# A selective scan on one core: order of the last-column copies, and a re-ordered opening of the stage

## The chip, the cores and the metric

The kernel runs on one core of a Trainium2 chip. The metric is the device time of one execution in microseconds (us). It was run three times: median 2136.71 us, from 2136.35 to 2136.91.

## The reference

A block of four layers over an input `x` of 4 × 1024 tokens of 128 features in float32; each adds its result to `x` and begins with a layer norm: windowed attention, a mixture of experts, a two-layer selective state-space model ("mamba"), and the mixture of experts once more. The change is in the third:

```python
def _mamba_layer(x, W_in, conv_w, conv_b, W_x, W_dt, b_dt, A_log, Dvec, W_out):
    xz = jnp.einsum('bld,ed->ble', x, W_in)
    u, z = jnp.split(xz, 2, axis=-1)                 # 256 channels each
    u = _silu(_causal_conv1d(u, conv_w, conv_b))     # 4 taps
    x_dbl = jnp.einsum('bld,rd->blr', u, W_x)
    dt, Bm, Cm = jnp.split(x_dbl, [DT_RANK, DT_RANK + D_STATE], axis=-1)
    dt = jax.nn.softplus(jnp.einsum('blr,dr->bld', dt, W_dt) + b_dt)
    A = -jnp.exp(A_log)                              # 16 states a channel
    # h_t = exp(dt A) h_(t-1) + dt B_t u_t ;  y_t = C_t h_t + D u_t
    y = _selective_scan(u, dt, A, Bm, Cm, Dvec)
    y = y * _silu(z)
    return jnp.einsum('bld,od->blo', y, W_out)
```

## The kernel before

**Units and steps.** `mamba()` cuts the work into 16 units: layer (2) × 512 tokens (`SEG`) × batch row (4), two units to a batch row, in the order of `UNITS`. The first three units are of the lower layer, then upper and lower alternate, and the last three are of the upper one. A unit holds its 256 channels as two halves `h` of 128 partitions. It has 16 steps, one for each state `n`; step `G` = 16 U + n. The second unit of a batch row starts from the last column that the first left for each state: `keep(U, n)` on ScalarE (L2174) copies the last columns of states n and n+1 out of the ring of 4 state buffers. So 8 of the 16 units (0, 1, 3, 5, 6, 8, 11, 13) keep columns, eight copies each.

**One step, by engine.** Each engine has its own hand-written order and waits for counting semaphores.
- VectorE: for each half a scan (`tensor_tensor_scan`, L2367) from a decay and a drive term, and for the driven states a product (L2347) for the next state's drive, in PSUM. Before the scans of step G it waits until state G−4 has been read by GpSimd and, in a unit that keeps columns, until the `keep` of state G−4 has been done. At step 4 (`BACK`) it makes the gating product of the unit before (L2372).
- ScalarE: exponentials `decays` (L2123), the copies out of PSUM, the softplus, the SiLU with a load of its table before and behind, and `scale` (L2146). In each step its order is: decays, copy of Y (step 3, L2153), convolution copies (steps 2 and 4, L2053), SiLU (step 4), the rows' copies (step 6), `soft` (step 9), gate copies (`gated`, L2110), `scale`, columns, and `keep` last.
- TensorE: the rows of B spread over the partitions (`rows_b`, L1865), or for 5 of the states the transposes of what ScalarE scaled (`upright`, L1890), or the diagonal form (state 11); the sum over states as transposes into Y (`accumulate`, L1919), which waits for GpSimd's product; for the next unit the convolution (L1823), gates (L1855), steps and transposes. The drive terms have two PSUM buffers (`PB`).
- GpSimd: the product of each state with C (L2313), two drives a unit for the states 4 and 12 (L2300), two products for the next unit's steps (L2321, L2324), and in units 0 to 5 the addition of the input.
- SyncE issues the transfers of B and C rows through DRAM.

**States by kind.** `AWAY` (4, 12): drive from GpSimd, decay in PSUM. `ACROSS` (2, 5, 8, 10, 14): scaled by ScalarE in the transposed layout and turned upright by TensorE. `DIAGONAL` 11. The eight others are driven: rows by TensorE, product by VectorE. `nth_drive`, `nth_upright`, `nth_across` and the lists `uses0` and `uses1` (who uses the two side banks, in order) count semaphores.

**The opening.** Before the loop, ScalarE takes the square root for the layer norm (`deviations`), the exponential of `decay`, the copies of unit 0's rows (`round_high(0)`), the softplus, and the first decays; TensorE the first rows, both gates, turns of B and delta_u, and half a convolution of unit 1.

## Time and profile before

| | us | share of the span |
|---|---|---|
| median of three runs | 2136.71 | |
| profiled execution | 2136.81 | |
| its span, first to last instruction | 2134.9 | |
| TensorE busy | 2000.8 | 94% |
| VectorE busy | 1473.7 | 69% |
| GpSimd busy | 1440.3 | 67% |
| ScalarE busy | 1205.7 | 56% |
| scan stage (first to last scan) | about 777 to 1575 | 37% |

The shares are means over stages with different limits; the stage in question has to be looked at by itself. Profile lines name the engine (PE TensorE, PEld its weight loads, DVE VectorE, ACT ScalarE, POOL GpSimd, SP SyncE), the line of the kernel (L2367), the operation, and what it writes and reads; many small buffers live in one tile called `experts`. In square brackets stands the idle time of the engine ahead of the group and what the profile takes for its releaser. Starts are counted from the span's start.

### The profile page before, as it was taken

To read this page: it belongs to the slowest core of one execution; us is meant where nothing else is said; L and a number is where in the kernel's file an instruction comes from. 1 tells how busy PE (TensorE), PEld (TensorE's weight loads), DVE (VectorE), ACT (ScalarE), POOL (GpSimd) and SP (SyncE) were. 2 spreads that over 40 slices of the span, in tenths; PEclk is the share of its full clock that TensorE was granted. 3 is DMA by queue.
4 is the path that set the end of the run, shared out by engine and by line. 5 is a ranking of instruction groups with operands and counts; after the bars stand their busy time and mean duration, and the time that the engine had idled before them with its cause. 6 is when DMAs were issued, how large, how long until landed. Compare 5 with 4: busy or idle time off the path is not lost. (4 is left out here: it accounts for less than half of the span.)

```text
span 2134.9 us, 42985 instructions
## 1 busy us (share of the span) xinstructions
PE 2000.8 (94%) x14574; PEld 1553.8 (73%) x14575; DVE 1473.7 (69%) x2717; ACT 1205.7 (56%) x2399; POOL 1440.3 (67%) x973
## 2 busy tenths in 40 slices
PE   7998999999999989899988898898789999999998
PEld 6886447999999636566666666566554499999994
DVE  6887684333333579999999999999976833333335
ACT  4775423322222269999999998999844232223222
POOL 5775005777767349999999999999950067777670
PEclk9999999999999999999999999999999999999999
DMA  8000100000001433333423333333234000000004
GB/s 307 1 0 2 40 1 18 25 25 26 25 23 26 116 98 96 105 107 99 110 99 110 101 100 106 103 98 105 95 129 156 2 22 26 25 26 25 25 24 122
DMA packets 83096, 146.44 MB, mean 69 GB/s; under 512 B 18555, under 2 KB 52349, under 8 KB 80806
## 3 DMA queue, kind: packets, MB, share of 16 engines
q1 hardware_dynamic: 73894, 126.36, 18.7%
q0 software_dynamic: 9088, 18.63, 3.2%
q8 instruction: 63, 1.03, 0.2%
q14 instruction: 51, 0.42, 0.1%
HBM read 128.04 MB, written 16.94 MB: 68 GB/s over the span
## 5 line engine op out<-in xcount | busy, mean ns | idle before, releaser
L2313 POOL TENSOR_TENSOR m_seen<-m_state,experts 128x1024 f32<-128x1024 f32 x256 | 599.9, 2362 | 45.1 <-DVE m_state L2367 24.8
L2367 DVE TENSOR_TENSOR_SCAN m_state<-experts,ps 128x512 f32<-128x512 f32 x448 | 537.2, 1233 | 1.7 <-issue 1.0
L2123 ACT ACTIVATE experts<-delta,experts 128x512 f32<-128x512 f32 x448 | 292.1, 714 | 1.0 <-DVE delta L2393 0.5
L1919 PE MATMUL ps<-ident,m_seen 128*128 128x128 f32 x2048 | 270.8, 276 | 12.9 <-POOL m_seen L2313 12.9
L1919 PEld LDWEIGHTS ps<-ident,m_seen 128*128 128x128 f32 x2048 | 239.8, 143 | 43.5 <-POOL m_seen L2313 20.6
L1596 POOL COPY f_weights<-experts 128x1898 f32 x142 | 252.1, 1775 | 23.9 <-issue 23.5
L1419 PE MATMUL first_up_ps<-f_xT,f_weights 128*128 128x128 f32 x1988 | 241.4, 275 | 1.7 <-issue 1.7
L1419 PE MATMUL ps<-zu,f_weights 128*128 128x128 f32 x1988 | 241.4, 275 | 1.7 <-issue 1.7
L1419 PEld LDWEIGHTS first_up_ps<-f_xT,f_weights 128*128 128x128 f32 x1988 | 233.2, 192 | 2.5 <-issue 2.5
L1419 PEld LDWEIGHTS ps<-zu,f_weights 128*128 128x128 f32 x1988 | 233.2, 192 | 2.5 <-issue 2.5
L2347 DVE TENSOR_TENSOR ps<-m_delta_u,ps 128x512 f32<-128x512 f32 x254 | 170.9, 673 | 5.6 <-PE ps L1865 5.6
L1584 POOL DMA_INDIRECT f_xin<-tokens,f_take x71 | 70.7, 996 | 151.4 <-DVE f_take L1123 132.9
L1584 POOL DMA_INDIRECT zu<-tokens,f_take x71 | 70.7, 995 | 147.2 <-DVE f_take L1123 128.6
L1168 DVE TENSOR_TENSOR first_hT<-first_gated,first_up_ps 128x512 f32<-128x512 f32 x71 | 48.9, 688 | 155.0 <-ACT first_gated L1274 151.2
L1168 DVE TENSOR_TENSOR zu<-zu,ps 128x512 f32<-128x512 f32 x71 | 48.8, 688 | 155.0 <-ACT zu L1274 151.2
L1274 ACT ACTIVATE first_gated<-first_up_ps 128x512 f32<-128x512 f32 x71 | 42.5, 599 | 194.7 <-PE first_up_ps L1419 194.7
L1274 ACT ACTIVATE zu<-ps 128x512 f32<-128x512 f32 x71 | 42.5, 598 | 194.7 <-PE ps L1419 153.8
L1890 PE MATMUL ps<-ident,experts 128*128 128x128 f32 x640 | 102.2, 284 | 41.4 <-DVE m_state L2367 36.5
L1890 PEld LDWEIGHTS ps<-ident,experts 128*128 128x128 f32 x640 | 73.1, 144 | 93.2 <-issue 85.6
L1475 PE MATMUL f_y_ps<-experts,first_hT 128*128 x1136 | 138.5, 275 | 0.5 <-DVE f_yout L1183 0.5
L1475 PE MATMUL ps<-experts,zu 128*128 x1136 | 138.5, 275 | 0.5 <-DVE delta L1183 0.5
L2146 ACT ACTIVATE experts<-experts 128x256 f32<-128x256 f32 x320 | 136.2, 498 | 0.7
(454 smaller groups left out, 4004.1 us busy)
## 6 DMA issues: line engine op xcount, KB each, us to landing
experts<-m_rows SPq DMA_DIRECT2D x144, 512.0 KB, 3.8
experts<-in_experts SPq DMA_DIRECT2D x17, 1461.0 KB, 18.2
tokens<-f_rows SPq DMA_DIRECT2D x8, 512.0 KB, 4.7
f_rows<-expert_out SPq DMA_DIRECT2D x8, 512.0 KB, 7.1
f_cols<-expert_out SPq DMA_DIRECT2D x8, 512.0 KB, 7.1
experts<-m_diagonal SPq DMA_DIRECT2D x16, 256.0 KB, 4.1
out<-X SPq DMA_DIRECT2D x4, 512.0 KB, 3.2
X<-in_x SPq DMA_DIRECT2D x4, 448.0 KB, 5.5
```

Source lines behind the costliest of these rows:

```text
L1168: dve.tensor_tensor(hT[:, s, A], gated[:, A], UP_A, ALU.mult).then_inc(s_hA, 1)
L1419: mm = pe.matmul(up_ps[:, bank + k, col:col + P], weights[:, s, at:at + P], xT[:, s, :], start=True, stop=True)
L1475: mm = pe.matmul(y_ps[:, 0:D], hT[:, 1 - s, c * P:(c + 1) * P], rhs, start=(c == 0), stop=(c == NC - 1))
L1584: pool.indirect_dma_start(xin[:, s, :], None, tokens_out[n], bass.IndirectOffsetOnAxis(ap=take[:, s:s + 1].bitcast(U32), axis=0)).then_inc ...
L1596: pool.tensor_copy(weights[:, s, :], experts[:, ds(where, GU)]).then_inc(s_weights, 1)
L1890: mm = pe.transpose(PB[n % B_RING][:, h, i * P:(i + 1) * P], scaled[:, nth_across[G] % SCALED, i, h * P:(h + 1) * P], ident[:])
L1919: mm = pe.matmul(Y[:, i // 2, at:at + P], seen[:, n % SEEN, h, i * P:(i + 1) * P], ident[:], is_transpose=True, start=(n == 0 and at == 0) ...
L2123: act.activation(PB[n % B_RING][:, h, :] if n in AWAY else dA[:, n % DECAYS, h, :], delta[:, U % 2, h, :], ACT.Exp, scale=decay[:, lhn:lhn ...
L2146: ins = act.activation(scaled[:, k % SCALED, i, :], across[:, i, :], ACT.Copy, scale=b_across[:, i * NS + n:i * NS + n + 1])
L2313: pool.tensor_tensor(seen[:, n % SEEN], state[:, n % RING], c_rep[:, Q % C_RING, n % C_GROUP, :].unsqueeze(1).to_broadcast([P, HALF, SEG]) ...
L2347: dve.tensor_tensor(PB[n % B_RING][:, h, :], delta_u[:, U % 2, h, :], PB[n % B_RING][:, h, :], ALU.mult).then_inc(s_drive, 1)
L2367: dve.tensor_tensor_scan(state[:, n % RING, h, :], decay_, drive_, before_, ALU.mult, ALU.add).then_inc(s_state, 1)
```

## The change

In the scan stage: `KEPT_FIRST = 10`. The `keep` that ScalarE issued at the end of an even step n is now issued at the beginning of that step if n ≥ 10 (so those of states 8 to 13), and stays where it was in the others.

In the opening: (a) ScalarE loads the table of the square root at once, copies unit 0's rows first, and then takes the square root and the exponential; VectorE's memset that this copy waits for comes first on VectorE. (b) State 2 of unit 0 is no longer of the scaled kind but driven by VectorE. (c) TensorE's two gates of unit 0, the turn of delta_u and the convolution of unit 1 stand in steps 0, 2 and 3 and no longer before the loop; ScalarE's gate copies are in steps 2 and 4, and the SiLU of unit 1 waits for them. The counts of `uses0`, `uses1` and of the waits follow.

```diff
+                KEPT_FIRST = 10
-                uses0 = [("turn", 1), ("gate", 0), ("b", 0), ("du", 0)]
-                uses1 = [("gate", 0), ("du", 0)]
+                uses0 = [("turn", 1), ("b", 0), ("du", 0)]
+                uses1 = [("du", 0), ("gate", 0)]
...
+                    if U == 0:
+                        uses0.append(("gate", 0))
...
-                scaled_states = [G for G in range(STEPS) if G % NS in ACROSS]
+                scaled_states = [G for G in range(STEPS) if G % NS in ACROSS and G != ACROSS[0]]
...
                         for h in range(HALF):
                             rows_b(0, h)
-                        for h in range(HALF):
-                            gate(0, h)
                         turn_b(0)
-                        turn_delta_u(0)
                         pe.wait_ge(s_hT, 1)
-                        convolve(1, *CONVOLVED[NS - 1])
...
-                                if n in CONVOLVED and n < NS - 1:
+                                if G == 0:
+                                    turn_delta_u(0)
+                                elif G == 2:
+                                    gate(0, 1)
+                                    convolve(1, 0, range(TAPS))
+                                if G and n in CONVOLVED and n < NS - 1:
                                     convolve(V, *CONVOLVED[n])
+                                if G == 3:
+                                    gate(0, 0)
...
-                        deviations(act, s_var, s_std)
+                        act.preload_act_table_set("sqrt_and_others")
...
+                            if V == 1:
+                                act.wait_ge(s_read0, nth0["gate", 0] + 1)
                             both = zu[:, V % 2]
...
+                        act.wait_ge(s_zero, 1)
+                        round_high(0)
+                        deviations(act, s_var, s_std)
                         act.preload_act_table_set("natural_log_exp_and_others")
                         act.activation(decay[:], decay[:], ACT.Exp).then_inc(s_exp_A, 1)
-                        act.wait_ge(s_zero, 1)
-                        round_high(0)
...
                         columns(1)
+                        columns_b(0)
                         act.wait_ge(s_neg_A, 1)
                         act.wait_ge(s_hT, 2)
                         decays(0)
                         decays(1)
-                        for h in range(HALF):
-                            gated(0, h)
-                        columns_b(0)
                         delta_u_across(0)
-                        scale(ACROSS[0])
+
+                        def keep_behind(U, n):
+                            done = (U, n - 2) if n else (U - 1, NS - 2)
+                            if n % 2 == 0 and done in nth_kept:
+                                keep(*done)
                         for G in range(STEPS):
...
+                            if n >= KEPT_FIRST:
+                                keep_behind(U, n)
...
                                     convolved(V, 1)
+                                    if U == 0:
+                                        gated(0, 0)
                                     silu(V)
...
+                            if G == 2:
+                                gated(0, 1)
...
-                            if n % 2 == 0 and ((U, n - 2) in nth_kept if n else (W, NS - 2) in nth_kept):
-                                keep(*((U, n - 2) if n else (W, NS - 2)))
+                            if n < KEPT_FIRST:
+                                keep_behind(U, n)
...
                     def _(dve):
+                        dve.memset(bc[2 * NS:2 * NS + DT_ROWS, :], 1.0).then_inc(s_zero, 1)
                         variances(dve, s_stats, s_var)
```

## Rows read from the trace of the kernel before

**Rows 1.** Busy us (count): PE PEld DVE ACT POOL, clock, DMA, GB/s; two units.

```profile
1230.00:1330.00 100.00, 89.97 (x543) 61.53 (x542) 99.97 (x106) 90.84 (x156) 93.94 (x41) 1.00 0.35 102
```

**Rows 2.** What VectorE waited for, 777 to 1576: us in total, times, longest.

```profile
DVE m_state L2367 <- POOL m_seen L2313: 22.7, 8, 2.8
...
DVE ps L2347 <- PE ps L1865: 5.6, 2, 4.9
```

**Rows 3.** Timeline of VectorE, unit 0: start, us, operation, count, idle before.

```profile
811.94 4.55 DVE L2367 TENSOR_TENSOR_SCAN m_state<-experts,ps 128x512 f32<-128x512 f32 x4 [0.18 <-issue]
...
819.34 1.22 DVE L2367 TENSOR_TENSOR_SCAN m_state<-ps,experts 128x512 f32<-128x512 f32 x1 [2.84 <-POOL m_seen L2313]
```

**Rows 4.** Timeline of ScalarE, unit 0.

```profile
814.42 1.28 ACT L2123 ACTIVATE ps<-delta,experts 128x512 f32<-128x512 f32 x2
...
819.05 0.20 ACT L2174 ACTIVATE experts<-m_state 128x4 f32<-128x4 f32 x1
```

**Rows 5.** Timeline of ScalarE, units 0 to 7, at its waits.

```profile
824.79 0.60 ACT L2047 ACTIVATE experts<-ps 128x512 f32<-128x512 f32 x1 [0.95 <-PE ps L1803]
...
887.43 1.02 ACT L2153 ACTIVATE experts<-ps 128x1024 f32<-128x1024 f32 x1 [1.17 <-PE ps L1919]
...
936.10 1.00 ACT L2153 ACTIVATE experts<-ps 128x1024 f32<-128x1024 f32 x1
...
973.00 0.60 ACT L2047 ACTIVATE experts<-ps 128x512 f32<-128x512 f32 x1 [1.41 <-PE ps L1803]
...
1085.16 0.21 ACT L2174 ACTIVATE experts<-m_state 128x4 f32<-128x4 f32 x1 [0.76 <-DVE m_state L2367]
...
1124.52 1.09 ACT L2136 ACTIVATE experts<-ps 128x512 f32<-128x512 f32 x2 [1.24 <-PE ps L1882]
...
1136.42 1.03 ACT L2153 ACTIVATE experts<-ps 128x1024 f32<-128x1024 f32 x1 [1.79 <-PE ps L1919]
```

**Rows 6.** Timeline of VectorE, gating products of units 2 and 3.

```profile
895.39 1.20 DVE L2372 TENSOR_TENSOR experts<-zu,ps 128x1024 f32<-128x1024 f32 x1
...
943.64 1.22 DVE L2372 TENSOR_TENSOR experts<-zu,ps 128x1024 f32<-128x1024 f32 x1 [0.58 <-PE ps L1941]
```

**Rows 7.** Timeline of TensorE, opening.

```profile
763.43 1.88 PE L1836 MATMUL ps<-experts,x_w 128*40 128x512 f32 x4 [1.02 <-PEq L966]
...
775.41 3.78 PE L1855 MATMUL ps<-experts,m_gateT_w 128*128 128x512 f32 x4 [1.22 <-ACT experts L2047]
```

**Rows 8.** Timeline of ScalarE, opening.

```profile
765.91 1.28 ACT L2189 ACT_TABLE_LOAD   x1
...
767.21 0.26 ACT L2190 ACTIVATE experts<-experts 128x64 f32<-128x64 f32 x1
...
767.37 0.57 ACT L2084 ACTIVATE experts<-ps 40x512 f32<-40x512 f32 x1
...
769.15 0.60 ACT L2196 ACTIVATE m_delta_u<-ps 128x512 f32<-128x512 f32 x1 [0.74 <-PE ps L1966]
...
774.24 0.63 ACT L2204 ACTIVATE m_delta_u<-m_delta_u 128x512 f32<-128x512 f32 x1
```

**Rows 9.** Timeline of VectorE, opening.

```profile
777.58 1.21 DVE L2367 TENSOR_TENSOR_SCAN m_state<-experts,ps 128x512 f32<-128x512 f32 x1
...
783.67 0.70 DVE L2347 TENSOR_TENSOR ps<-m_delta_u,ps 128x512 f32<-128x512 f32 x1 [4.88 <-PE ps L1865]
```

**Rows 10.** Timeline of GpSimd, its first drive.

```profile
778.17 2.35 POOL L2300 TENSOR_TENSOR experts<-m_delta_u,experts 128x1024 f32<-128x1024 f32 x1 [6.46 <-DMA experts<-m_rows]
```

**Rows 11.** Busy times as in rows 1, two pieces of the opening.

```profile
772.00:774.00 2.00, 1.80 (x6) 0.72 (x6) 0.28 (x1) 1.95 (x4) 0.00 (x0) 0.50 0.34 97
...
780.00:782.00 2.00, 1.61 (x10) 1.19 (x11) 0.00 (x0) 1.15 (x3) 0.52 (x1) 1.00 0.91 293
```

**Rows 12.** Timeline of ScalarE, first convolution copy of unit 1.

```profile
790.08 0.67 ACT L2053 ACTIVATE zu<-ps,experts 128x512 f32<-128x512 f32 x1
```

**Rows 13.** Busy times as in rows 1, units 1 to 5.

```profile
831.83:1079.38 247.55, 224.59 (x1343) 156.39 (x1342) 237.47 (x251) 236.59 (x431) 238.89 (x106) 0.99 0.35 103
```

More of the change, by code:

```diff
@@ L1712, in tokens, with scaled_before @@
                     return (t // C * STREAMS + s) * TPB + t % C * TILES
+                def scaled_before(V):
+                    return len(ACROSS) * V - 1 if V else 0
                 def stored(V):
@@ L1752, in mamba @@
                 nth_decay = {G: k for k, G in enumerate(decayed)}
-                driven = [G for G in range(STEPS) if G % NS not in AWAY + ACROSS + (DIAGONAL,)]
-                nth_upright = {G: k for k, G in enumerate(G for G in range(STEPS) if G % NS in ACROSS + (DIAGONAL,))}
-                scaled_states = [G for G in range(STEPS) if G % NS in ACROSS]
-                nth_across = {G: k for k, G in enumerate(G for G in range(STEPS) if G % NS in ACROSS)}
+                scaled_states = [G for G in range(STEPS) if G % NS in ACROSS and G != ACROSS[0]]
+                nth_across = {G: k for k, G in enumerate(scaled_states)}
+                nth_upright = {G: k for k, G in enumerate(G for G in range(STEPS) if G in nth_across or G % NS == DIAGONAL)}
+                driven = [G for G in range(STEPS) if G % NS not in AWAY and G not in nth_upright]
                 nth_drive = {G: k for k, G in enumerate(driven)}
@@ L2084, in round_high @@
                             act.activation(bc[0:XR], SIDE1[0:XR], ACT.Copy).then_inc(s_bc, 1)
-                            wait(act, s_b, (V - 1) * (NS - len(AWAY) - len(ACROSS) - 1) * HALF)
+                            wait(act, s_b, ((V - 1) * (NS - len(AWAY) - len(ACROSS) - 1) + 1) * HALF if V > 1 else 0)
                             act.activation(parts[0:32, V % 2, :], SIDE1[0:32], ACT.Copy).then_inc(s_rounded, 1)
@@ L2126, in columns_b @@
                             act.wait_ge(s_side0, nth0["b", V] + 1)
-                            wait(act, s_scaled, len(ACROSS) * V)
+                            wait(act, s_scaled, scaled_before(V))
                             act.activation(b_across, SIDE0[:, 0:TILES * NS], ACT.Copy).then_inc(s_read0, 1)
                         def delta_u_across(V):
-                            wait(act, s_scaled, len(ACROSS) * V)
+                            wait(act, s_scaled, scaled_before(V))
                             if V:
@@ L2356, in scan @@
                             else:
-                                if n in ACROSS or n == DIAGONAL:
+                                if G in nth_upright:
                                     dve.wait_ge(s_upright, nth_upright[G] * HALF + h + 1)
@@ L2383, in add_out @@
                                     row_sums(dve, at + i)
-                        dve.memset(bc[2 * NS:2 * NS + DT_ROWS, :], 1.0).then_inc(s_zero, 1)
                         normalise(1)
```

## The prediction

> **What bounds the kernel now.** I read the 40 slices of the page first: the scan stage fills 777 to 1576 us, and only there do four engines stand at 9 tenths together. Everything the diff touches runs in it or in the 14 us that open it. The busy times of one inner stretch come next [rows 1]: of 100 us VectorE works 99.97, ScalarE 90.8, GpSimd 93.9, TensorE 90.0. So VectorE sets the pace, and the others follow within 6 to 10%. Its list of waits [rows 2] has two items that matter: eight waits of 2.8 us (22.7 together) ahead of a scan, and 4.9 us ahead of one drive product. The rest of its time is work, but for 0.6 us ahead of two gating products, which tell something further down.
>
> The profile puts the eight waits down to GpSimd. I don't follow it. In unit 0 the scan of state 12 begins at 819.34, though its predecessors ended at 816.50 [rows 3]; ScalarE's copy of last columns runs from 819.05 to 819.25 [rows 4] and the scan starts 0.09 behind it, whereas the GpSimd product that frees the ring slot is the one on state 8, three products earlier. By the code, state 12 overwrites state 8 and must wait for `keep(U, 8)`, and only the 8 units that have a successor in their batch row keep anything: eight units, eight waits. The decays of state 12 were begun at 814.42 [rows 4], so they are not late: written by 815.7, or 3.6 ahead of the scan.
>
> **Part 1: copies first.** `keep(U, 8)` moves from behind the decays of 12 and 13, the gate copy and the `scale` (814.42 to 819.05, 4.6 us) to ahead of them. State 9, for which it waits, ended at 811.9, where the four scans of states 10 and 11 begin [rows 3], and ScalarE is there at 814.4. It costs 0.1 us more ahead of the decays, which have 3.6 − 2.84 = 0.8 us to spare afterwards. So each wait goes: 8 × 2.84 = 22.7 us at VectorE. `keep(U, 10)` and `keep(U, 12)` go ahead of work too; ScalarE comes to them at about 3 and 6 us behind the start of scan 12, while states 11 and 13 end 0 and 5.7 us behind it, so I cost them at nothing. The cover of the second is thin: 0.3 us.
>
> What is late next? ScalarE. The gating product of a unit's step 4 hangs on a ScalarE chain (copy of Y, `scale`, decays 4 and 7, convolution copy) and TensorE's turn behind it; in unit 3 the copy of Y began at 936.10 and the gating product at 943.64, 7.54 later and after a wait of 0.58; in unit 2 7.96 lie between 887.43 and 895.39, without a wait [rows 5, 6]. So a lateness beyond 0.4 us is passed on one to one. So between step 7 of a kept unit and step 3 of the next, ScalarE must be able to give up the same 2.84. What it can give up is its idle time there [rows 5]:
> - Kept units 6, 8, 11, 13, whose successor begins with no such debt: 1.24 (waiting for the turned delta_u) + 1.79 (waiting for Y) = 3.03, more than 2.84. Full gain, 4 × 2.84 = 11.36.
> - Unit 1: 1.17 ahead of the copy of Y at 887.43, and 0.42 that the gating product of unit 2 has to spare there (7.96 − 7.54). Gain 1.59.
> - Unit 3: 1.41 ahead of the column copy at 973.00; of sparing room in unit 4 I count none, as ScalarE is late there already. Gain 1.41.
> - Unit 5: 0.76 ahead of 1085.16. Gain 0.76.
> - Unit 0: 0.95 ahead of 824.79; its rest depends on part 2.
> Units 0 to 5 also normalise and transpose inputs on ScalarE (2.2 us), which is why they have less.
>
> **Part 2: the opening.** TensorE has the rows of unit 0 ready at 765.31 [rows 7]; ScalarE copies them at 767.37, behind Sqrt, a table load and Exp [rows 8]. First in line the copy starts at 765.35 and its second half ends at 766.4; Sqrt follows at 766.3 (VectorE's variance is put off by the 0.48 memset ahead of it, to 766.1), the load of the table ends at 767.85, Exp at 768.1. The first Abs then starts at 768.05 to 768.1 instead of 769.15, and the waits for TensorE's subtractions vanish, so that the last Ln starts at 772.1 instead of 774.24 [rows 8]: 2.1 us. The first scan moves from 777.58 to 775.5 [rows 9]. SyncE's queue doesn't gain: its copy of the rows waits for the diagonal's transfer, not for ScalarE, so GpSimd's first drive stays at 778.17, where it waits for that transfer's successor [rows 10].
>
> On the load of the table row and rule differ. The load at 765.91 took 1.28 and the Exp behind it began at 767.21, 0.02 later [rows 8]. The Trainium skill (ScalarE: Activation LUTs, What ACT_TABLE_LOAD costs) adds some 1.38 us of drain to each such load. By that rule the load, which now stands on the way to the first Abs, would leave 0.7 of the 2.1 us, and the forecast would be 2122.4; the trace does not bear it out.
>
> Next, VectorE's wait of 4.88 behind the first scan [rows 9]: TensorE still had gates (3.78 us, rows 7), turns and a convolution in front of the second state's rows. They move into steps 0 to 3, and state 2 of unit 0 is driven: minus one `scale` of 1.6 on ScalarE, minus 8 transposes, plus 2 matmuls of rows and 2 products of 0.58 on VectorE. A scan is 1.14 [rows 3] and a product 0.58, so the second scan of state 1 ends at 775.5 + 4 × 1.14 + 3 × 0.58 = 781.8, and VectorE alone would be through state 3 at 788.1.
>
> But the work comes back in step 2: TensorE must see the second half of state 1 end (781.8, and a tenth for the signal) before row 3's second half; then 2 + 8 matmuls of the gate and the four taps stand in a row, and ScalarE waits for them in `convolved(1, 0)`. ScalarE gets there at 784.4. At full clock the ten take 0.43 each (the first four of the stage, 1.88, less 0.17 of filling) and end at 786.9; at half clock 0.86 (the four gate matmuls from 775.41, 3.78) [rows 7]. The granted clock was 0.50 at 772 to 774 and 1.00 from 780 [rows 11], 4.6 us after the gates had begun to fill the engine. The new opening leaves TensorE emptier up to 782, so I take half clock until 786.8: the taps end at X = 789.0. Today ScalarE makes that copy at 790.08 [rows 12]; up to its table load behind the SiLU it now also has two gate copies (1.0) and 0.5 of waiting for the second half's taps and gate. ScalarE is thus 790.1 − 789.0 − 1.5 = −0.4 us ahead, that is, 0.4 behind; at full clock 1.7 ahead. With the 0.95 us of unit 0 it carries 0.6 us (2.7) of gain into the gating product of unit 1, and that is what units 0 and 1's beginning are worth, since VectorE waits there for whatever it had in hand.
>
> **Sum.** 0.6 + 1.59 + 1.41 + 0.76 + 11.36 = 15.7 us. The profiled execution took 2136.81 us (span 2134.9), 0.1 above the median: 2136.81 − 15.7 = 2121.1, and 2121.0 against the median. At full clock it would be 2118.9.
>
> **The rivals.**
> - **ScalarE has more to give than its idle time shows** (its waits shift, its order absorbs). Then VectorE keeps up to 4.6 in unit 0's second half with its wait, and all of its waits in 1, 3 and 5: 4.6 + 8.5 + 11.4 = 24.5, or 2112.3. GpSimd would just allow it: in units 1 to 5 it works 238.9 of 247.6 us [rows 13], as much as VectorE does without three waits (239.0), and in unit 0 its first product may follow the first drive at once, at 780.5 [rows 10]. For it: TensorE's half clock behind the stalls made some of ScalarE's lateness. Against: the wait of 0.58 at 943.64 [rows 6], which shows no slack at all.
> - **Units 1, 3 and 5 give nothing**, since GpSimd or ScalarE is full there: 11.4 remains, 2125.4. For it: ScalarE works 236.6 of the 247.6 us of units 1 to 5 [rows 13], 47.3 a unit, and a kept unit is to take VectorE 32 × 1.14 + 16 × 0.58 + 1.1 = 46.9.
> - **The profile's releaser is right**, and the copy is not what scan 12 waits for. Then only the opening counts: 2136, no change. Against: 0.09 us in rows 3 and 4, and the number of kept units.
> - **Slower.** Moved to the head of steps 10, 12 and 14, the copies make ScalarE wait in its queue for the second half of the state before, with the decays of 14 and 16, columns and the turned delta_u behind it. Where ScalarE comes early, it falls into step with VectorE and can't lay up time for the SiLU and its two table loads. It decides once the wait is over 1 us at both of the later copies, that is, if ScalarE comes over 1 us earlier than I have it: 16 waits of 1.5 are 24 against 15.7, or 2145.
>
> **How the numbers follow.** Forecast case 0.60 (its own range 2117 to 2124, from the two clocks and ±2 for units 0 to 6), more to give 0.18, nothing from 1, 3 and 5 0.14, releaser right 0.04, slower 0.04. A range of 2112 to 2127 leaves out the last two and the edges of the others, some 0.13. The measurement can tell 0.2% (4.3 us) from no change: faster 0.92, same 0.04, slower 0.04.
>
> **What would show it.** Right: no wait of VectorE ahead of scan 12 in any unit, the copy of last columns ahead of the decays; waits of about 1 to 2 us at line 2372's product in units 1, 2, 4 and 6; full VectorE from unit 7 on. First scan at 775.5, the 4.88 gone, and instead ScalarE idle by 2 to 5 us ahead of `convolved(1, 0)` at a granted clock of 0.5. Wrong: waits ahead of the copies at lines 2174, scans waiting for GpSimd's products, a granted clock of 1.0 at 782 (then 2 us less), or waits at the gating product that are missing (then up to 8 us less) or found behind unit 7 as well.

## The result and the profile after

| | before | after |
|---|---|---|
| median, us (runs) | 2136.53 (4 runs, 2133.23 to 2136.91) | 2120.95 (4 runs, 2114.74 to 2122.90) |
| ratio to before, 95% interval | | 0.9925 [0.9902, 0.9949] |
| profiled execution, its span | 2136.81, 2134.9 | 2114.74, 2112.6 |
| start of the stage's opening (ScalarE's first table load) | 763.39 | 759.36 |
| from there to the end of the last scan | 811.38 | 793.08 |
| behind it | 560.12 | 560.12 |

The forecast was 2121.0. The change is faster by 15.6 us in the medians. The two profiled executions differ by 22.3 us of span; 4.0 of them lie ahead of the opening, where nothing was changed. The stage itself is shorter by 18.3. Below, "from the opening" counts from ScalarE's first table load, so that the 4.0 us drop out.

Busy time, from the page of after: VectorE works 3.5 us more than before, so what was won is waiting, not work.

```profile
PE 1993.2 (94%) x14568; PEld 1548.9 (73%) x14569; DVE 1477.2 (70%) x2719; ACT 1199.7 (57%) x2395; POOL 1438.9 (68%) x973
```

What VectorE waited for in the stage of after (us in total, times, longest), against [rows 2]:

```profile
DVE m_state L2390 <- ACT ps L2135: 3.8, 1, 3.8
DVE experts L2395 <- PE ps L1948: 3.1, 5, 0.9
DVE ps L2370 <- PE ps L1872: 2.2, 6, 0.6
DVE m_state L2390 <- PE ps L1897: 1.4, 1, 1.4
DVE m_state L2390 <- issue: 1.1, 1, 1.1
```

The item of 22.7 us has gone, and the name of GpSimd with it. New are 3.8, 1.4 and 1.1 us ahead of scans 4, 5 and 6 of unit 0. The waits ahead of the gating products (L2395) are 3.1 us in this list, none over 0.9. Four of the six waits ahead of drive products (L2370) are of 0.32 us, close to the end of units 0, 1, 3 and 5: there TensorE comes late with the rows, behind its transposes of the inputs that ScalarE's normalisation releases. The run e9, which cuts the normalisation, doesn't have them.

ScalarE in unit 0 of after, against [rows 4]: the copy of last columns (0.21 us) stands ahead of the decays of state 12.

```profile
810.65 0.21 ACT L2186 ACTIVATE experts<-m_state 128x4 f32<-128x4 f32 x1
810.76 1.28 ACT L2135 ACTIVATE ps<-delta,experts 128x512 f32<-128x512 f32 x2
```

VectorE there, against [rows 3]: six scans in a row, then that of state 12 with nothing ahead of it.

```profile
805.61 7.02 DVE L2390 TENSOR_TENSOR_SCAN m_state<-experts,ps 128x512 f32<-128x512 f32 x6
...
812.54 1.20 DVE L2390 TENSOR_TENSOR_SCAN m_state<-ps,experts 128x512 f32<-128x512 f32 x1
```

The opening on ScalarE, against [rows 8, 12]: the rows' copy first (761.37), the load of the logarithm's table, the exponential 0.02 us behind its end, and far down a wait of 4.16 ahead of the first convolution copy of unit 1.

```profile
759.36 1.28 ACT L2050 ACT_TABLE_LOAD   x1 [0.26 <-PEq L966]
...
761.37 0.59 ACT L2096 ACTIVATE experts<-ps 40x512 f32<-40x512 f32 x1 [0.73 <-PE ps L1843]
...
762.57 1.28 ACT L2204 ACT_TABLE_LOAD   x1
...
763.87 0.26 ACT L2205 ACTIVATE experts<-experts 128x64 f32<-128x64 f32 x1
...
784.32 0.69 ACT L2063 ACTIVATE zu<-ps,experts 128x512 f32<-128x512 f32 x1 [4.16 <-PE ps L1830]
```

The opening on VectorE, against [rows 9]: first scan at 771.50, which is 12.14 from the opening (before: 14.19). The wait of 4.88 behind it is gone, but in its place three waits lie ahead of scans 4, 5 and 6.

```profile
771.50 1.21 DVE L2390 TENSOR_TENSOR_SCAN m_state<-experts,ps 128x512 f32<-128x512 f32 x1
...
787.88 2.34 DVE L2390 TENSOR_TENSOR_SCAN m_state<-ps,experts 128x512 f32<-128x512 f32 x2 [3.81 <-ACT ps L2135]
...
791.62 1.22 DVE L2390 TENSOR_TENSOR_SCAN m_state<-experts,ps 128x512 f32<-128x512 f32 x1 [1.40 <-PE ps L1897]
...
796.54 1.22 DVE L2390 TENSOR_TENSOR_SCAN m_state<-experts,ps 128x512 f32<-128x512 f32 x1 [1.14 <-issue]
```

TensorE there: gate and taps stand in a row. The chain is taps (780.01 to 784.28), ScalarE's copy at 784.32, behind it in ScalarE's queue a gate copy, a copy of last columns, `scale` (1.70) and the decays of state 4 (from 787.08), and scan 4 at 787.88.

```profile
778.30 1.91 PE L1862 MATMUL ps<-experts,m_gateT_w 128*128 128x512 f32 x2
...
780.01 4.27 PE L1830 MATMUL ps<-experts 128*128 128x512 f32 x8
```

Two pieces of the opening and units 1 to 5 of after (columns as in [rows 1]): the granted clock was 0.50 (1.2 of 2.4 GHz) until 781.4, in the middle of the taps, 22.0 from the opening; and in 241.5 us VectorE works 237.9, GpSimd 238.7, ScalarE 234.8 [rows 13].

```profile
779.00:781.00 2.00, 2.00 (x4) 0.81 (x3) 2.00 (x3) 1.16 (x2) 2.00 (x1) 0.50 0.52 207
...
782.00:784.00 2.00, 2.00 (x6) 0.73 (x4) 2.00 (x2) 0.00 (x0) 1.76 (x1) 1.00 0.67 260
...
825.43:1066.90 241.47, 222.56 (x1343) 153.20 (x1342) 237.85 (x251) 234.79 (x430) 238.73 (x106) 1.00 0.33 106
```

Worked out from the starts of the gating products, each counted from the opening, the 18.3 us came in like this:

| won between | predicted | measured |
|---|---|---|
| opening and gating product of unit 1 | 0.6 | 1.42 |
| from there to that of unit 2 | 1.59 | 2.27 |
| to that of unit 4 | 1.41 | 2.27 |
| to that of unit 6 | 0.76 | 1.56 |
| to the end of the last scan | 11.36 | 10.79 |
| sum | 15.7 | 18.3 |

### The profile page after: what moved, and what is told of

It is laid out like the page before. It is cut to its first block and busy times, and to the rows that moved or that the text cites. A ratio compares the mean times of both kernels' runs of the same rounds, so it can differ in the third digit from the quotient of the medians.

```text
span 2112.6 us, 42970 instructions
## 1 busy us (share of the span) xinstructions
PE 1993.2 (94%) x14568; PEld 1548.9 (73%) x14569; DVE 1477.2 (70%) x2719; ACT 1199.7 (57%) x2395; POOL 1438.9 (68%) x973
## 5 line engine op out<-in xcount | busy, mean ns | idle before, releaser
L2335 POOL TENSOR_TENSOR m_seen<-m_state,experts 128x1024 f32<-128x1024 f32 x256 | 599.7, 2372 | 27.6 <-DVE m_state L2390 14.2
L1926 PE MATMUL ps<-ident,m_seen 128*128 128x128 f32 x2048 | 271.7, 276 | 20.3 <-POOL m_seen L2335 19.9
L1419 PE MATMUL first_up_ps<-f_xT,f_weights 128*128 128x128 f32 x1988 | 241.4, 275 | 1.7 <-issue 1.7
L1419 PE MATMUL ps<-zu,f_weights 128*128 128x128 f32 x1988 | 241.4, 275 | 1.7 <-issue 1.7
L2370 DVE TENSOR_TENSOR ps<-m_delta_u,ps 128x512 f32<-128x512 f32 x256 | 173.0, 676 | 2.4 <-PE ps L1872 2.2
L1475 PEld LDWEIGHTS f_y_ps<-experts,first_hT 128*128 128x128 f32 x1136 | 132.4, 192 | 0.7 <-issue 0.7
L1475 PEld LDWEIGHTS ps<-experts,zu 128*128 128x128 f32 x1136 | 132.4, 192 | 0.7 <-issue 0.7
```

Source lines behind the costliest of these rows:

```text
L1419: mm = pe.matmul(up_ps[:, bank + k, col:col + P], weights[:, s, at:at + P], xT[:, s, :], start=True, stop=True)
L1475: mm = pe.matmul(y_ps[:, 0:D], hT[:, 1 - s, c * P:(c + 1) * P], rhs, start=(c == 0), stop=(c == NC - 1))
L1926: mm = pe.matmul(Y[:, i // 2, at:at + P], seen[:, n % SEEN, h, i * P:(i + 1) * P], ident[:], is_transpose=True, start=(n == 0 and at == 0) ...
L2335: pool.tensor_tensor(seen[:, n % SEEN], state[:, n % RING], c_rep[:, Q % C_RING, n % C_GROUP, :].unsqueeze(1).to_broadcast([P, HALF, SEG]) ...
L2370: dve.tensor_tensor(PB[n % B_RING][:, h, :], delta_u[:, U % 2, h, :], PB[n % B_RING][:, h, :], ALU.mult).then_inc(s_drive, 1)
```

## The experiments

"Won at unit 1" is how much earlier than before, from the opening, the first scan of unit 1 starts; "won in the stage" is the same for the end of the last scan; "half clock" is when, from the opening, the clock of 0.50 that reigns in it ended in the profiled execution.

| run | median, us | ratio, interval | won at unit 1 | won in the stage | half clock until |
|---|---|---|---|---|---|
| after | 2120.95 | 0.9925 [0.9902, 0.9949] | 2.36 | 18.30 | 22.0 |
| e0_change_again | 2121.83 | 0.9924 [0.9910, 0.9938] | 0.90 | 14.2 | 24.7 |
| e1_copies_first | 2123.12 | 0.9925 [0.9911, 0.9939] | 0.98 | 16.85 | 18.1 |
| e2_opening | 2138.33 | 1.0005 [0.9996, 1.0014] | −1.60 | −1.08 | 24.8 |
| e3_taps_split | 2116.24 | 0.9903 [0.9888, 0.9918] | 6.33 | 21.04 | 14.1 |
| e4_split_opening_alone | 2135.39 | 0.9990 [0.9981, 0.9999] | 1.94 | 0.63 | 21.3 |
| e5_filler | 2119.69 | 0.9925 [0.9908, 0.9943] | 3.16 | 18.58 | 20.3 |
| e6_rows_first | 2134.74 | 0.9987 [0.9978, 0.9997] | 2.21 | 0.98 | 13.7 |
| e7_copy_before_silu | 2117.51 | 0.9908 [0.9893, 0.9923] | 5.89 | 19.71 | 18.8 |
| e8_small_add | 2112.91, one run | | 5.12 | 22.16 | 20.2 |
| e9_short_norm | 2114.36, one run | | 6.75 | 22.67 | 14.1 |
| e10_copies_and_rows | 2117.14 | 0.9910 [0.9894, 0.9927] | 4.68 | 19.6 | 14.1 |

**The change again.** No edit.

> The changed kernel once more, since its four runs lay 8 us apart (2114.7 to 2122.9). Of the 22.1 us by which its profiled run is shorter than that of before, 4.0 lie ahead of the scan stage, where nothing was changed. My theory: the stage itself is worth 18.3 us each time (from the stage's first load of a table on ScalarE to the last scan, 811.4 us before, 793.1 after), and the rest is spread of the other stages, which the kernel before has too (2133.2 to 2136.9). So a ratio of 0.991 to 0.9935, and a stage of 792 to 795 us in this profile also where the whole run is slower. Rival: the changed kernel has gained a spread of its own inside the scan stage (its granted clock fell to 0.5 in five late windows of 3.4 us that the kernel before does not have), and then the stage's length in this profile differs from 793 by several us.

The median agrees (2121.83), but the profiled stage lasted 797.16, outside 792 to 795. It is 4.1 us longer than in the first profile, so the rival holds. In this execution the half clock ended at 24.7, the wait ahead of scan 4 of unit 0 was 5.03, and 1.5 of the 4.1 us were lost by unit 1; another 0.9 went in unit 9 and 1.6 ahead of the gating product in unit 15. So one profile of the stage is good to some 4 us, and the 18.3 of the first is not more right than the 14.2 of this one.

**Part 1 alone.**

```diff
+                KEPT_FIRST = 10
...
+                            if n >= KEPT_FIRST:
+                                keep_behind(U, n)
...
-                            if n % 2 == 0 and ((U, n - 2) in nth_kept if n else (W, NS - 2) in nth_kept):
-                                keep(*((U, n - 2) if n else (W, NS - 2)))
+                            if n < KEPT_FIRST:
+                                keep_behind(U, n)
```

> The kernel before with part 1 alone: the copies of last columns first from step 10 on. My theory, with the shortest way from the copy of Y to the gating product corrected from 7.54 to 6.87 us (the changed kernel's trace): unit 0 gives 1.5 (ScalarE idle 0.95, 0.57 to spare), units 1, 3, 5 some 2.5, 2.5 and 1.8 as in the changed kernel, units 6, 8, 11, 13 2.84 each: 19.7 us of the stage, ratio 0.9908, with waits ahead of the gating product in units 1, 2, 4 and 6 and none ahead of scan 12 anywhere. Rival 1 (VectorE alone sets the time): 22.7 us. Rival 2 (the profile's releaser, GpSimd, is right for scan 12): nothing.

VectorE's waits in the stage, from its list:

```profile
DVE ps L2356 <- PE ps L1866: 6.5, 6, 4.9
...
DVE experts L2381 <- PE ps L1942: 3.9, 5, 1.0
```

No wait ahead of scan 12 is left; the 4.9 of the opening is as before, and the gating products wait as in after (0.86, 0.15, 0.57 in units 1, 2 and 3). Won were 16.85, not the 19.7 expected. 1.62 of the difference is the first scan, which came later than before (15.81 against 14.19 from the opening): here the four step matmuls, too, ran at half clock. TensorE's timeline:

```profile
770.42 3.78 PE L1967 MATMUL ps<-experts,dt_w 9*128 9x512 f32 x4 [2.67 <-ACT experts L2085]
```

Before, the same four took 2.13. Most of the rest went late in the stage, 1.02 in a wait ahead of the gating product in unit 15. In the medians part 1 alone is as fast as the whole change: 0.9925 both.

**Part 2 alone.**

```diff
-                KEPT_FIRST = 10
+                KEPT_FIRST = 16
```

> The changed kernel with its copies of last columns where they were, that is, part 2 alone. My theory: ScalarE is the bound of unit 0; the four taps' convolution copy comes 1.7 us earlier than before but two gate copies and 0.7 us of waiting are put behind it, so the scan of state 12 in unit 0, which again waits for the copy of last columns in ScalarE's queue, is at most 0.5 us earlier counted from the stage's start, and so is everything behind it: 0 to 0.5 us, ratio 0.9995 to 1.000. Rival (VectorE's opening counts): the first scan 2.05 earlier and the 4.88 wait gone, less 1.2 of products: 5.7 us, ratio 0.9973.

VectorE's waits:

```profile
DVE m_state L2390 <- POOL m_seen L2335: 22.9, 8, 3.2
...
DVE m_state L2390 <- ACT ps L2135: 5.1, 1, 5.1
```

The eight waits are back, and the opening gives nothing: at unit 1 the kernel is 1.6 us behind before. The wait of 5.1 is the one on the decays of state 4 behind the taps' copy, for which ScalarE idled 5.49 us. So the expected 0 to 0.5 us was missed on the losing side; the place was right, for ScalarE's decays of state 12 start 52.64 from the opening, 1.61 later than before, and all behind them is later by as much. Parts 1 and 2 add up to 15.8 us in the stage, between the two profiles of the whole.

**Taps split.** This asks where the opening's gain goes: at unit 1's gating product, as I had it, or in unit 0's steps 4 to 6. Half of the taps go ahead of step 2, and the gate now stands behind the other half and no longer ahead of the taps.

```diff
-                                elif G == 2:
-                                    gate(0, 1)
-                                    convolve(1, 0, range(TAPS))
+                                elif G == 1:
+                                    convolve(1, 0, (0, 1))
+                                elif G == 2:
+                                    convolve(1, 0, (2, 3))
+                                    gate(0, 1)
```

> The changed kernel with the first half's four taps of unit 1 split: two in step 1, where TensorE is idle behind the rows of state 2, two in step 2 ahead of the gate. My theory: TensorE ends the taps 1.5 to 2.5 us earlier (781.8 to 782.8 instead of 784.3 in the changed kernel's profile, counted from the same stage start), ScalarE's wait of 4.16 shrinks by as much, and since ScalarE binds up to the gating product of unit 1 the whole stage does too: 1.5 to 2.5 us less than the changed kernel, 790.6 to 791.6 us of stage. Rival (the rows of state 3, which now stand behind two taps, hold VectorE up, or the gain is lost at the next unit's gating product): no gain, 793 us or more.

TensorE in two pieces of four, each at full clock, and ScalarE's copy with no wait ahead of it; a window of the opening at clock 1.00:

```profile
777.58 1.88 PE L1830 MATMUL ps<-experts 128*128 128x512 f32 x4
...
780.99 1.88 PE L1830 MATMUL ps<-experts 128*128 128x512 f32 x4
```

```profile
782.93 0.68 ACT L2065 ACTIVATE zu<-ps,experts 128x512 f32<-128x512 f32 x1
```

```profile
779.00:782.00 3.00, 1.91 (x7) 0.82 (x6) 3.00 (x5) 3.00 (x7) 3.00 (x3) 1.00 0.91 272
```

VectorE: scan 4 without a wait, scan 5 still with 1.32, and the gating products of units 1 and 3 with the same waits as in after.

```profile
786.86 2.31 DVE L2392 TENSOR_TENSOR_SCAN m_state<-ps,experts 128x512 f32<-128x512 f32 x2
...
790.50 1.22 DVE L2392 TENSOR_TENSOR_SCAN m_state<-experts,ps 128x512 f32<-128x512 f32 x1 [1.32 <-PE ps L1897]
...
838.78 1.22 DVE L2397 TENSOR_TENSOR experts<-zu,ps 128x1024 f32<-128x1024 f32 x1 [0.85 <-PE ps L1948]
...
934.81 1.22 DVE L2397 TENSOR_TENSOR experts<-zu,ps 128x1024 f32<-128x1024 f32 x1 [0.56 <-PE ps L1948]
```

6.33 us are won at unit 1, and the lead of 4.0 over after is kept through its gating product: the wait there is 0.85 in both kernels. The stage took 790.34, 2.7 less than in the first profile of after and a little more than the 1.5 to 2.5 expected; here the clock was back at 14.1, so not all of it is the split. Both engines of the chain, not VectorE alone, come earlier. So much of what the opening had lost in after was lost in steps 2 to 6 of unit 0; of it, the waits of 1.32 and 1.15 ahead of scans 5 and 6 are still there. By its median this is the fastest version that leaves nothing out, 4.7 us below the change; the intervals of the two ratios overlap by 0.0016.

**Split opening, copies last.** The edit of e3 with `KEPT_FIRST = 16`.

> The split-taps kernel (e3) with its copies of last columns where they were: the mended opening alone. In e3 unit 1 began 6.33 us earlier than in the kernel before, counted from the stage's start, in e1 (copies alone) 0.98; in e2 (the change's own opening alone) 1.60 later. Theory A (the opening and the copies add up, and what spoilt the opening is only the time of the four taps): 6.33 - 0.98 = 5.3 us earlier at unit 1 and to the end, ratio 0.9975. Theory B (ScalarE's queue binds up to the copy of last columns in unit 0, as I had it in the prediction, and only both parts together free it): under 3 us, ratio above 0.9985.

ScalarE and VectorE at state 12 of unit 0, from the timeline:

```profile
813.13 1.28 ACT L2137 ACTIVATE ps<-delta,experts 128x512 f32<-128x512 f32 x2
...
817.76 0.20 ACT L2188 ACTIVATE experts<-m_state 128x4 f32<-128x4 f32 x1
...
818.04 1.22 DVE L2392 TENSOR_TENSOR_SCAN m_state<-ps,experts 128x512 f32<-128x512 f32 x1 [2.82 <-POOL m_seen L2337]
```

The decays of state 12 start 49.08 from the opening against 51.03 before, and the whole unit gains just that: 1.94. Theory B holds. With the copy last, VectorE waits at scan 12 for ScalarE's queue, and what the opening gave VectorE beyond ScalarE's own 1.95 is taken back there. That is why part 2 by itself shows at unit 1 as nothing but ScalarE's own time: 1.95 won with the taps split, 1.60 lost without.

**Filler.** Nine matmuls with no use, in the change's opening, into a bank that is overwritten later, to see whether a busier TensorE gets its full clock sooner.

```diff
+                        def filler(count):
+                            for _ in range(count):
+                                pe.matmul(Y[:, 0, :], spread[:, 0:P], spread[:, 0:SEG], start=True, stop=True)
+                        filler(3)
                         turn_b(0)
...
+                            if G in (1, 2):
+                                filler(2)
+                            if G == 1:
+                                filler(2)
```

> The changed kernel with nine more matmuls of 128x128 weights over 512 bf16 columns on TensorE before step 3, where it is idle (three ahead of the turn of B, two between and two behind the rows of state 2, two between the rows of state 3); they write the bank of Y, whose first accumulation overwrites them. Theory A (the half clock is the price of an opening that leaves TensorE thin): the granted clock is back at 1.00 before the taps begin, 15 us behind the stage's start, the taps' copy on ScalarE runs at 22.0 to 23.0 us behind the stage's start instead of 24.96, and unit 1 begins 2 to 3 us earlier than in the changed kernel (gain of 4.4 to 5.4 against before, instead of 2.36 and 0.90 in its two profiles). Theory B (the clock comes back late whatever stands there, and the taps' place in the queue is the cause): no change, or later by the 0.4 to 1.5 us that the nine take on the way.

```profile
784.10 0.69 ACT L2072 ACTIVATE zu<-ps,experts 128x512 f32<-128x512 f32 x1 [3.31 <-PE ps L1830]
```

Half clock until 20.3, taps' copy at 24.14 from the opening (after: 24.96). The full clock came back sooner than in after, but not ahead of the taps, and e1, without a filler, had it at 18.1. With that spread nothing follows about the filler.

**Rows first, alone.** Before, with piece (a) only: `round_high(0)` ahead of `deviations`, and the memset first on VectorE.

```diff
+                        act.wait_ge(s_zero, 1)
+                        round_high(0)
                         deviations(act, s_var, s_std)
```

> The kernel before with the first piece of the opening alone: unit 0's rows copied ahead of the square root and the exponential, gates and convolution where they were, state 2 scaled. The first scan should begin at 12.15 us behind the stage's start instead of 14.19, as in the change. Theory A (all of TensorE's and ScalarE's work up to the second state hangs on these copies): 1.6 to 2.0 us at unit 1 and at the end, ratio 0.9991. Theory B (GpSimd's first drive, tied to the rows' transfer, or a clock that falls earlier takes it back): under 0.5 us.

```profile
DVE m_state L2369 <- POOL m_seen L2314: 22.6, 8, 2.8
...
DVE ps L2349 <- PE ps L1865: 5.1, 2, 4.8
```

2.21 won at unit 1, about the 2.04 by which the first scan is earlier, through the wait of 4.8 that stays. That is as much as the whole change has there (2.36 and 0.90). To the end 0.98 are left: 0.8 went in unit 8, with half clock at 1170.0 to 1173.5 and 1214.4 to 1217.8, and 0.5 in unit 15.

**Copy before the SiLU.** e3, with the copy of states 2 and 3 in step 4 ahead of the SiLU.

```diff
+                                    keep_behind(U, n)
                                     silu(V)
...
-                            if n < KEPT_FIRST:
+                            if n < KEPT_FIRST and (n != SILU or V == N_UNITS):
                                 keep_behind(U, n)
```

> The split-taps kernel (e3) with the copy of the last columns of states 2 and 3 ahead of the SiLU and its two table loads in step 4, instead of behind them. In e3 scan 6 of unit 0 waits 1.15 us, 0.09 behind the end of that copy, as scan 12 did before. Theory A (same form of wait, nothing else late): 1.1 us at unit 1 and at the end, stage 789.2 against 790.34 but for clock windows late in the stage, no wait ahead of scan 6. Theory B: the matmuls for states 5 and 6, 0.9 to 1.3 late in e3, put a wait in its place, and unit 1 gains under 0.4.

```profile
798.92 1.22 DVE L2393 TENSOR_TENSOR_SCAN m_state<-experts,ps 128x512 f32<-128x512 f32 x1 [0.51 <-issue]
...
805.35 1.22 DVE L2393 TENSOR_TENSOR_SCAN m_state<-experts,ps 128x512 f32<-128x512 f32 x1 [0.68 <-issue]
```

The wait of 1.15 ahead of scan 6 has gone, and 0.51 and 0.68 ahead of scans 8 and 10 stand for it. The number is Theory B's (unit 1 wins 5.89, against 6.33 in e3, with the clock back 4.7 later), its cause is not: in ScalarE's timeline two further copies of last columns, of states 4 to 7, end at 798.82 and 805.26, and scans 8 and 10 begin 0.10 and 0.09 behind them. So it is the same form of wait again, one step on each time. That wait was only the first place at which ScalarE's lateness in unit 0 showed; moving one copy of 0.2 us does not cure it.

**Less on GpSimd.** e3, where GpSimd adds 16 of the 512 columns of the input in units 0 to 5; the other 496 are left out. One run.

```diff
-                            pool.tensor_tensor(X[:, at:at + SEG], X[:, at:at + SEG], xn[:], ALU.add).then_inc(s_added, 1)
+                            pool.tensor_tensor(X[:, at:at + 16], X[:, at:at + 16], xn[:, 0:16], ALU.add).then_inc(s_added, 1)
```

> The split-taps kernel (e3) with GpSimd's addition of the input to the residual (step 12 of units 0 to 5 and twice ahead of the loop) cut to 16 of 512 columns: the rest of that sum is left out. It takes some 1.1 us off GpSimd in each of units 0 to 5. Theory A (the waits of 0.57 ahead of the gating product in units 3 and 5 come from GpSimd's product for the unit's first states, behind which TensorE's turn of Y is queued; those of 0.86 in units 1 and 6 from ScalarE, late with the copy of Y): 0.57 gone in units 3 and 5, 0.86 left in units 1 and 6, about 1.1 us off the stage. Theory B (all of them are ScalarE's, as I had it in the prediction): all four stay.

The gating product of unit 3:

```profile
933.00 1.20 DVE L2397 TENSOR_TENSOR experts<-zu,ps 128x1024 f32<-128x1024 f32 x1
```

The wait of 0.56 is gone there and in unit 5, and stays in units 1 and 6 (0.85, 0.86); units 1 to 5 take 240.07 instead of e3's 241.44. So in units 3 and 5 it is GpSimd that was waited for, by way of TensorE. In unit 1 TensorE now idles ahead of the turn of Y and starts it 0.09 behind the end of ScalarE's copy (836.43): there ScalarE ends last.

```profile
836.52 1.06 PE L1948 MATMUL ps<-ident,experts 128*128 128x128 f32 x8 [0.95 <-ACT zu L2065]
```

TensorE's queue in after and in before shows how GpSimd comes in: the turn of Y stands behind an `accumulate` that waits for GpSimd's product.

```profile
931.17 1.09 PE L1926 MATMUL ps<-ident,m_seen 128*128 128x128 f32 x8 [0.64 <-POOL m_seen L2335]
...
934.86 1.04 PE L1948 MATMUL ps<-ident,experts 128*128 128x128 f32 x8
```

```profile
938.87 1.09 PE L1919 MATMUL ps<-ident,m_seen 128*128 128x128 f32 x8 [0.65 <-POOL m_seen L2313]
```

Of these two fences the first is after, the second before.

**Less on ScalarE.** e3, where ScalarE normalises one of the four tiles in units 0 to 5; three are left out. One run.

```diff
-                            for i in range(TILES):
+                            for i in range(1):
```

> The split-taps kernel (e3) with ScalarE's normalisation of the inputs (step 12 of units 0 to 5) cut to one tile of four: the other three keep old values. It takes some 1.2 us off ScalarE in each of units 0 to 5. Theory A: the waits of 0.86 ahead of the gating product go in units 1 and 6, those of 0.15 in units 2 and 4 too, those of 0.57 in units 3 and 5 stay; 1.7 to 2.0 us off the stage. Theory B (all are ScalarE's): the 0.57 go as well, 3.1 off. Theory C (GpSimd is full through units 1 to 5, idle for 2.8 of 285 us in e3, and holds the length of those units whatever ScalarE does): the waits move elsewhere and under 0.8 is gained.

```profile
839.71 1.22 DVE L2397 TENSOR_TENSOR experts<-zu,ps 128x1024 f32<-128x1024 f32 x1 [1.07 <-PE ps L1948]
...
935.70 1.22 DVE L2397 TENSOR_TENSOR experts<-zu,ps 128x1024 f32<-128x1024 f32 x1 [0.59 <-PE ps L1948]
```

ScalarE's copy of Y in unit 1 came 1.14 us earlier from the opening than in e3 (68.55, 69.69), and yet the waits at the gating products grew (units 1 to 6: 1.07, 0.50, 0.59, 0.53, 0.56, 1.12); units 1 to 5 won 0.26 us. GpSimd, idle 2.4 us of their 241.2, holds the stage there: Theory C. (In e3 it is 2.8 of 241.4, not of 285 as the expectation has it.) The turn of Y in unit 1 starts 0.98 behind the end of ScalarE's copy, where it was 0.10 in e3, because 3.70 us before it TensorE waited for GpSimd's product:

```profile
834.94 1.09 PE L1926 MATMUL ps<-ident,m_seen 128*128 128x128 f32 x8 [0.77 <-POOL m_seen L2337]
```

In e3 the same matmuls began at 833.77, so GpSimd's way alone would have let the turn begin at 837.47, by this estimate, and it began at 837.68. So there the two ways are nearly of one length, ScalarE's the longer by 0.2 us, and relieving either alone can't give much. The stage as a whole is 1.6 us shorter than e3's, but only 0.5 of that by the gating product in unit 10; the rest lies behind, where the half clocks fall at other places in the two profiles.

**Copies and rows.** Part 1 with piece (a), without (b) and (c): e1 and e6 together.

> The kernel before with copies of last columns first (part 1) and unit 0's rows copied first, but gates, convolution and state 2 as they were: the change without the pieces (b) and (c) of the opening. By the pieces: first scan 2.0 earlier (e6), unit 0 shorter by 2.6 as in e1 (54.25 to 51.63), so unit 1 begins 4.6 us earlier than before, against 2.36 and 0.90 in the change's two profiles and 6.33 in e3; then as the change does, so 2 to 3.5 us faster than the change: ratio 0.991. Rival (VectorE needs the gates out of the way as well, and ScalarE gives nothing back without them): unit 1 at 2.4 or less, ratio 0.9925 as in the change.

```profile
DVE ps L2358 <- PE ps L1866: 7.8, 8, 4.8
```

4.68 us are won at unit 1 against 2.36 and 0.90 of the whole change, with the wait of 4.8 in place. So pieces (b) and (c) as they stand cost 2.3 to 3.8 us there (the half clock, which ended 8 to 11 us sooner, is part of it), and only with the taps split do they give more than they take (e3: 6.33, at the same clock). The medians don't separate these three: 0.9910 here, 0.9903 in e3 and 0.9925 for the change have intervals that overlap.

## Why the prediction was right, and where it was not

**The total** (2121.0 against 2120.95) is closer than its steps deserve, and that is luck. The stage won 18.3 in one profile and 14.2 in the other; the steps sum to 15.7. The rivals fall. "Releaser right" and "slower" fall by the times; "nothing from 1, 3 and 5" by the 6.1 us that came in there; "more to give" came true in part only, since up to unit 6 there came in 3.2 us more than I had summed (1.7 in the repeat), where that rival needs 8.8.

**The eight waits** were right: place, releaser and price. The decays' 0.8 us to spare held, as scan 12 waits nowhere, and the copies at the head of steps 12 and 14 cost nothing. Before, all eight of these scans start 0.09 behind the end of ScalarE's copy. Against the profile's own releaser, e1 alone shows it: only the copies moved, and all eight waits went. e2 brings them back, 22.9 us.

**ScalarE and what it can give up.** The mechanism was right, two sizes were off.
- The shortest way from the copy of Y to the gating product was taken as 7.54, from unit 3, because a wait of 0.58 ended it. It is 6.88: in after 833.01 to 839.89 in unit 1, and 880.79 to 887.67 in unit 2. This is the term that was mis-sized. The wait of 0.58 was put down to ScalarE, but e8 shows that GpSimd's product ends last there. Each gating product had 0.66 more to spare than I counted, 1.08 and not 0.42 in unit 2.
- ScalarE's small waits: in unit 1 before there were also 0.48 us at 851.77 ahead of the rows' copy. I counted only the 1.17 ahead of the copy of Y.

With these, unit 2 comes out: 0.86 (below) + 1.17 + 0.48 + 1.08 = 3.59; at its gating product 1.42 + 2.27 = 3.69 were measured. ScalarE before, and the two lines of after that carry the 6.88:

```profile
851.77 0.59 ACT L2084 ACTIVATE experts<-ps 40x512 f32<-40x512 f32 x1 [0.48 <-PE ps L1836]
```

```profile
833.01 1.01 ACT L2165 ACTIVATE experts<-ps 128x1024 f32<-128x1024 f32 x1
```

```profile
839.89 1.22 DVE L2395 TENSOR_TENSOR experts<-zu,ps 128x1024 f32<-128x1024 f32 x1 [0.85 <-PE ps L1948]
```

Units 3 and 5 gained 0.86 and 0.80 more than predicted. Most of that is the first term alone: the way from the copy of Y to the gating product fell from 7.68 to 6.87 in unit 4, where I had counted no room at all, and from 7.54 to 6.87 in unit 6. The second gave nothing there, as the small waits ahead of the rows' copy stay about as they were (in unit 3 0.59 before, 0.42 in after; in unit 5 0.58 and 0.73). As a sign I had named waits of 1 to 2 us at the gating products in units 1, 2, 4 and 6; they are 0.85, 0.14, 0.15 and 0.85, and 0.56 and 0.59 in units 3 and 5 besides.

What lies behind unit 6's gating product gave 0.6 less than 11.36: between gating products, units 6, 8 and 11 gave 2.92, 2.97 and 2.94, but from unit 12's to the end of the stage only 2.02 came in, with half clock at both ends of unit 13 (1402.6 to 1406.0, 1450.4 to 1453.8) and waits of 0.30, 0.30 and 0.58.

**The first scan** moved by 2.04 (predicted 2.1), and e6 carries it by itself. On the table load the row decided against the rule: the exponential starts 0.02 us behind the 1.28 us of the load at 762.57, on the critical way now. The Trainium skill (ScalarE: Activation LUTs, What ACT_TABLE_LOAD costs) would have some 1.38 us of drain there; no run here shows it, and this row contradicts it.

**The opening behind it.** Predicted: 4.88 gone, a wait of 2 to 5 us of ScalarE ahead of the taps' copy, at a clock of 0.50. Found: 4.16, the clock back at 22.0 in the middle of the taps. The copy came 24.96 from the opening, where I had 25.6. ScalarE's copy of Y in unit 1 came 0.86 earlier (73.65 against 74.51), predicted 0.55; with 0.56 from the way behind it (7.44 before, 6.88 now) this makes the 1.42.

Wrong was where VectorE gives its gain back. I let it keep it to unit 1's gating product. It loses it at once, at scans 4, 5 and 6 (3.81, 1.40, 1.14 in after). The first is because the decays of state 4 stand behind the taps' copy in ScalarE's queue (2.8 us behind it); the other two wait for TensorE's transposes of state 5 and, behind the SiLU, for a copy of last columns. For the total it makes no difference, as ScalarE carried the sum. For the conclusion it does: I read the loss as ScalarE's load through unit 0 and 1, and in good part it is one row of ten matmuls in the wrong place. e3, without it, has won 6.33 at unit 1, against 2.36 in after and 0.90 in e0. What is clock in this can be told from kernels with the same order: without the split, the wait ahead of scan 4 was 2.98 (with the fillers), 3.81, 5.03 and 5.13 for half clocks that ended at 20.3, 22.0, 24.7 and 24.8; with it, none, 0.37, 1.05 and 1.47 for 14.1, 18.8, 20.2 and 21.3. Either row rises by some 0.45 to 0.48 us per us, and at equal clock they lie 1.9 apart: by that estimate the split itself is worth 1.9 of scan 4's wait, the rest is clock. Whether the order of work sets when the clock comes back stays open: e3, e6, e9 and e10 had it by 14.1, but e7, e8 and e4, with e3's opening, at 18.8, 20.2 and 21.3. The same four had also lost it last, at 6.9 to 7.3 from the opening; e7, e8 and e4 lost it at 5.2, 6.6 and 4.2. These three have the very opening of e3 and e9, so the order of work alone does not set when the clock falls.

## What to carry to other kernels

A tiny copy at the end of an engine's in-order queue can be the thing that a neighbour waits for, and the profile may name another engine for it: compare the end of each candidate with the start of the waiter, and count how often the wait occurs against how often each candidate exists. When a wait goes, what the next engine can give is its idle time up to the next common point, every small piece of it; and a wait that is taken as proof of no slack must first be followed through all engines that feed it. Work that is moved off a start must not come back as one long row ahead of something that the pacing engine needs.

## What the runs showed of the hardware that I had not expected

- The opening's half clock ended between 13.7 and 24.8 us from its start in thirteen profiles, and for one kernel (after and its repeat) at 22.0 and 24.7. It falls on a chain that sets the time: between these two profiles of one kernel, 2.7 us of it cost 1.5 us at unit 1. Later stretches at half clock, of 3 to 10 us, come at places that differ between profiles of the same kernel (643.2 and 691.0 from the opening in after, 451.4, 645.9 and 693.7 in its repeat).
- The part ahead of the stage, the same in all kernels, ended between 759.4 and 765.8, and that behind it took 560.1 or 561.7 us. Two profiles are to be compared stage by stage, each from its own start.
- ScalarE, GpSimd and VectorE are so near each other in units 1 to 5 that relieving GpSimd of its addition gave 1.4 us and ScalarE of three quarters of its normalising 0.3.
